# Perceiver layer on one Trainium2 core: shared expert with stationary weights, expert weights halved in place, fp32 down weights

## The reference

```python
x = x + cross_attention(layernorm(x), ctx, ctx)   # 16 heads of 16, 257 keys
x = x + attention(layernorm(x))                   # normalised weights, q and k; mixed with its input
x = x + moe(layernorm(x))

def moe(xt):                                      # xt [1024, 256]
    logits = xt @ gate_w.T                        # 8 experts
    idx = top_k(logits + beta, 2)
    c = scatter(sigmoid(logits[idx]))
    g = xt @ gate_proj_w[e]; u = xt @ up_proj_w[e]     # [256, 512] each
    eo = (silu(g) * u) @ down_proj_w[e]                # [512, 256]
    shared = (silu(xt @ shared_gate_w) * (xt @ shared_up_w)) @ shared_down_w
    return sum_e(c_e * eo_e) + shared
```

## Time and profile before

| | us |
|---|---|
| median of 3 runs (lowest, highest) | 446.9 (444.79, 455.19) |
| the profiled execution's own time | 446.99 |
| its span, first to last instruction | 445.2 |
| busy: TensorE matmuls | 366.0 |
| busy: GpSimd | 248.3 |
| busy: VectorE, ScalarE | 235.3, 235.2 |

### The profile page before, as it was taken

How to read it: one execution, slowest core, us unless ns; L and a number is a source line. 1 busy time by engine, 2 the same in 40 slices (tenths; PEclk the granted TensorE clock), 3 DMA queues, 4 the chain that set the end, 5 groups by cost and what they waited for, 6 DMA issues and landing times.

```text
span 445.2 us, 8817 instructions
## 1 busy us (share of the span) xinstructions
PE 366.0 (82%) x3020; PEld 245.2 (55%) x3020; DVE 235.3 (53%) x498; ACT 235.2 (53%) x478; POOL 248.3 (56%) x316
## 2 busy tenths in 40 slices
PE   4679978989898879788579676777779999999991
PEld 3356646667675556555467563443435656556660
DVE  1744456556555864686763746965642333333330
ACT  3546875757676666675585753455432332333330
POOL 4258588988765984855253515577293233242332
PEclk9979999999999998998898888999998999999998
DMA  7444958595779878566912112068742434454231
GB/s 221 148 93 92 179 124 174 122 173 130 156 195 219 193 166 203 121 131 130 353 50 96 49 49 78 17 205 285 245 87 51 62 49 64 57 61 61 39 35 24
DMA packets 110570, 55.54 MB, mean 125 GB/s; under 512 B 85920, under 2 KB 104352, under 8 KB 110528
## 3 DMA queue, kind: packets, MB, share of 16 engines
q1 hardware_dynamic: 106336, 49.66, 48.1%
q0 software_dynamic: 4192, 5.32, 7.6%
HBM read 21.51 MB, written 9.33 MB: 69 GB/s over the span
## 4 chain that ended last, share of the span: by engine, by line
PE 27%; DVE 22%; DMA 21%; ACT 13%; issue 11%; POOL 5%; POOLq 0%; SPq 0%; ACTq 0%; DVEq 0%
PE bank L1203 18%; DMA out<-yrow,info 18%; PE quad L1203 6%; ACT prob L605 4%; DVE cat L784 3%; ACT kT L584 2%; DMA pT<-p 2%; DVE negmax L815 2%; POOL wdn L477 2%; DVE qm L802 2%; ACT v_hi L513 2%; DVE qk L784 2%; DVE wgu L921 1%; POOL p L423 1%; DVE v_lo L784 1%
## 5 line engine op out<-in xcount | busy, mean ns | idle before, releaser
L605 ACT ACTIVATE prob<-quad,negmax 128x257 f32<-128x257 f32 x128 | 54.1, 481 | 49.2 <-DVE negmax L815 48.8
L423 POOL TENSOR_TENSOR p<-prob,p 128x512 f16<-128x512 f32 x64 | 72.8, 1138 | 5.3
L506 POOL DMA_INDIRECT out<-yrow,info x23 | 36.0, 1564 | 70.6 <-DMA out<-yrow,info 60.4
L420 POOL TENSOR_SCALAR p<-prob 128x512 f16<-128x512 f32 x64 | 41.3, 645 | 49.9 <-DMA pT<-p 30.5
L1203 PE MATMUL quad<-wgu,xT 128*128 x276 | 63.8, 381 | 1.5 <-issue 1.1
L784 DVE TENSOR_TENSOR v_lo<-bank,v_hi 128x512 f16<-128x512 f32 x32 | 22.1, 691 | 61.1 <-ACT v_hi L513 61.1
L1203 PE MATMUL bank<-cT,wk 128*128 128x257 f32 x128 | 43.6, 430 | 7.5 <-DMA cT<-in_ctxT 5.9
L1203 PE MATMUL quad<-kT,qm 64*128 64x257 f32 x256 | 44.6, 428 | 3.5 <-ACT prob L605 3.5
L815 DVE TENSOR_REDUCE negmax<-quad 128x2 f32<-128x514 f32 x64 | 42.5, 684 | 6.2 <-PE quad L1203 6.2
L784 DVE TENSOR_TENSOR hT<-bank,hT 128x512 f16<-128x512 f32 x31 | 21.4, 690 | 44.0 <-ACT hT L513 44.0
L1203 PEld LDWEIGHTS quad<-wgu,xT 128*128 128x128 f16 x276 | 26.8, 98 | 32.1 <-issue 6.7
(11 more groups left out here) (206 smaller groups left out, 743.1 us busy)
## 6 DMA issues: line engine op xcount, KB each, us to landing
wide<-un SPq DMA_DIRECT2D x32, 132.0 KB, 2.9
cT<-in_ctxT SPq DMA_DIRECT2D x8, 514.0 KB, 4.1
wst<-in_L_ffn_gate_proj_w SPq DMA_DIRECT2D x8, 512.0 KB
wst<-in_L_ffn_up_proj_w SPq DMA_DIRECT2D x8, 512.0 KB
wst<-in_L_ffn_down_proj_w SPq DMA_DIRECT2D x8, 512.0 KB
routed_rows<-pad_row SPq DMA_DIRECT2D x1, 3036.0 KB, 12.8
pT<-p SPq DMA_TRANSPOSE x64, 3.5
out<-acc SPq DMA_DIRECT2D x8, 128.0 KB
```

Source lines behind the costliest of these rows:

```text
L420: pool.tensor_scalar(out=p16[n % 2][:, h, 0, :, :], in0=prob[n % 4][:, h2, 0:256], scalar1=1.0, scalar2=0.0, op0=ALU.mult, op1=ALU.add).th ...
L423: pool.tensor_tensor(out=p16[n % 2][:, h, 1, :, :], in0=prob[n % 4][:, h2, 0:256], in1=p16[n % 2][:, h, 0, :, :], op=ALU.subtract).then_in ...
L506: pool.indirect_dma_start(out, bass.IndirectOffsetOnAxis(ap=info[n % NR][:, 0:1].bitcast(I32), axis=0), yrow[n % 2][:, :], None, compute_o ...
L605: act.activation(prob[m % 4][:, g, :], quad[:, g, 0:LK], ACT.Exp, bias=negmax[m % 4][:, g:g + 1]).then_inc(exps, 1)
```

## The change

1. The four staging buffers go. There are 18 slots `wslot` of 4 KB a partition; the fp32 gate or up chunk c is loaded into slot c + 2 and its two fp16 halves are written to slot c. The shared gate and up use `sslot` in the same way. All 16 gate and up chunks are halved by ScalarE (`high`) and VectorE (`w_low`), two in each of the 8 shared tiles; the shared ones during the self attention. GpSimd halves nothing.
2. Down weights, routed (`wdn`) and shared (`sdn`), stay fp32 and are loaded straight to their place. `down` is 4 fp32 matmuls of 256 columns.
3. Shared tiles: the weights are stationary and the tokens stream, in 4 blocks of 128 hidden columns, 6 matmuls of 128 columns each, so that `hid` comes out transposed and is itself the stationary operand of `down`. No turn, no copy.
4. Routed tiles: up and turn as before; ScalarE copies the turned tile once, as fp32, and VectorE's low half goes.
5. `xr16` is filled by eight transposing DMAs of SyncE from `x16` (`rows_back`) instead of 16 GpSimd instructions.
6. Loads: two in the attention loop; ten and the pad write from its end; six after the last cross-attention tile; the eight downs after the rows.
7. Order: on TensorE the logits of all tiles stand ahead of the first shared half; `down(q)` stands ahead of `up_half(q + 2)`; on VectorE `up(q + 2)` stands last in a shared tile's turn. `od` moves from wide to qm. R, PARTS and NJ are 128, 1 and 23: the tiling of routed rows is unchanged.

```diff
-        wdn = sb("wdn", [P, NE, 2, 4, E], F16, sc)
+        wdn = sb("wdn", [P, NE, 4, E], F32, sc)
-        wst = [sb(f"wst{i}", [P, 2 * M], F32, sc) for i in range(NC)]
+        wslot = sb("wslot", [P, 2 * NE + 2, 2, 2, M], F16, sc)
+        sslot = sb("sslot", [P, 4, 2, 2, M], F16, sc)
+        sdn = sb("sdn", [P, 4, E], F32, sc)
...
+                def gate_up(c):
+                    e, n = divmod(c, 2)
+                    w = a[("L0_ffn_gate_proj_w", "L0_ffn_up_proj_w")[n]][e].rearrange("(k p) m -> p k m", p=P)
+                    sp.dma_start(whole(wslot[:, c + 2, :, :, :]).rearrange("p (k m) -> p k m", k=2), w).then_inc(ld_u[c // 4], 16)
+                def rows_back(q):
+                    sp.wait_ge(xl_ok, 2 * q + 2)
+                    for a_ in range(2):
+                        for k in range(2):
+                            sp.dma_start(xr16[:, 4 * q:4 * q + 4, a_ * E + k * P:a_ * E + (k + 1) * P], x16[a_][:, k, 4 * q * P:(4 * q + 4) * P],
+                                         transpose=True).then_inc(xr_in, 16)
...
-                    if 16 <= n < 20:
-                        expert_part(n - 16)
-                    elif 22 <= n < 25:
-                        expert_part(n - 18)
+                    if n in (24, 26):
+                        shared_part((n - 24) // 2)
+                for c in range(4):
+                    gate_up(c + 12)
+                sp.wait_ge(U_ps, B)
+                for c in range(5):
+                    gate_up(c)
+                sp.dma_start(sdn[:, :, :], ...).then_inc(ld_sd, 16)
+                for j in range(4):
+                    sp.wait_ge(un_out[j], 16 * NT)
+                gate_up(5)
                 sp.wait_ge(pool_k, 2)
                 sp.dma_start(xs_dram.rearrange("(j p) e -> p j e", p=P), ...).then_inc(xs_pad, 16)
+                sp.wait_ge(WO_ps, NT)
+                for c in range(6, 12):
+                    gate_up(c)
+                rows_back(0)
+                sp.wait_ge(W2_ps, NT)
+                rows_back(1)
+                for e in range(NE):
+                    sp.dma_start(wdn[:, e, :, :], ...).then_inc(ld_wd, 16)
...
-                for t in range(NT):
-                    pool.wait_ge(n3_rows, t + 1)
-                    pool.tensor_scalar(out=xr16[:, t, 0:E], in0=xn[:, t, :], ...)
-                    pool.wait_ge(row_hi, t + 1)
-                    pool.tensor_tensor(out=xr16[:, t, E:2 * E], ...)
+                pool.wait_ge(xr_in, 16 * 8)
...
+                def high(c):
+                    if c % 4 == 0:
+                        act.wait_ge(ld_u[c // 4], 64)
+                    wait(act, w_lo, c - 1)
+                    act.activation(halves(wslot[:, c, :, :, :], 0), whole(wslot[:, c + 2, :, :, :]), ACT.Copy, scale=SH).then_inc(w_hi, 1)
...
                 for q in range(NT + TILES):
+                    if q + 2 < NT:
                         silu(q + 2)
+                    if q < NT:
+                        high(2 * q)
+                        high(2 * q + 1)
...
                 for q in range(NT + TILES):
                     if q < NT:
+                        w_low(2 * q)
                         y_(q)
+                        w_low(2 * q + 1)
                     if 0 <= q + 1 - NT < TILES:
                         sel_(q + 1 - NT)
+                    if q + 2 < NT:
+                        up(q + 2)
+                    elif NT <= q + 1 < NT + TILES:
+                        up(q + 1)
...
+                        for c in range(4):
+                            cols = slice(c * P, (c + 1) * P)
+                            i = 0
+                            for k in range(2):
+                                for a_, w_ in ((0, 0), (1, 0), (0, 1)):
+                                    last = mm(dst[:, cols], sslot[:, n, w_, k, cols], x16[a_][:, k, q * P:(q + 1) * P], i == 0, i == 5)
+                                    i += 1
...
+                    for c in range(4):
+                        if q < NT:
+                            last = mm(bank[6 + s][:, 0:E], hid[s][:, c * P:(c + 1) * P], sdn[:, c, :], c == 0, c == 3)
+                        else:
+                            w = wdn[:, bass.ds(te[q - NT][0], 1), c, :].rearrange("p a n -> p (a n)")
+                            last = mm(bank[6 + s][:, 0:E], hT[s][:, c * P:(c + 1) * P], w, c == 0, c == 3)
...
-                lg_(4)
-                lg_(5)
+                for t in range(4, NT):
+                    lg_(t)
                 up_half(0, 0)
-                lg_(6)
-                lg_(7)
...
                     down(q)
+                    if q + 2 < NT:
+                        up_half(q + 2, 0)
+                        up_half(q + 2, 1)
+                    elif q == NT - 1:
+                        expert(0)
+                        up_half(NT, 0)
+                        up_half(NT, 1)
```

More of the change, by code:

```diff
@@ L170, in perceiver_kernel @@
         acc = sb("acc", [P, NT, E], F32, sc)
-        hT = [sb(f"hT{i}", [P, 2, 4, P], F16, sc) for i in range(2)]
         yrow = [sb(f"yrow{i}", [P, E], F32, sc) for i in range(2)]
@@ L174, in perceiver_kernel @@
         hid = [sb(f"hid{i}", [P, M], F32, sc) for i in range(2)]
+        hT = [sb(f"hT{i}", [P, M], F32, sc) for i in range(2)]
         sb("spacer", [P, 376], F32, sc)
@@ L256, in vt_bank, with halves, whole @@
             return bank[(3, 3, 7, 6)[p]]
-        def gate_up(c):
-            return (NE - 1, c - 3) if c < 5 else divmod(c - 5, 2)
-        def by_pool(c):
-            return POOL_LO[0] <= c < POOL_LO[1] or POOL_LO[2] <= c
-        def nth(c):
-            return sum(by_pool(i) == by_pool(c) for i in range(c + 1))
-        def half(c, i):
-            if c < 2:
-                return sgu[:, c, i, :, :].rearrange("p k m -> p (k m)")
-            if c == 2:
-                return sdn[:, i, :, :].rearrange("p k m -> p (k m)")
-            if c >= 19:
-                return wdn[:, c - 19, i, :, :].rearrange("p k m -> p (k m)")
-            e, n = gate_up(c)
-            return wgu[:, e, n, i, :, :].rearrange("p k m -> p (k m)")
+        def halves(slot, i):
+            return slot[:, i, :, :].rearrange("p k m -> p (k m)")
+        def whole(slot):
+            return slot.rearrange("p i k m -> p (i k m)").bitcast(F32)
         def n3_bank(p):
@@ L465, in _ @@
                         bias(t + 1)
-                def halves(c):
-                    if c == 5:
-                        pool.wait_ge(U_ps, B)
-                    elif c == 11:
-                        pool.wait_ge(WO_ps, NT)
-                    pool.wait_ge(w_sc, nth(c))
-                    pool.tensor_copy(half(c, 0), wst[c % NC][:, :]).then_inc(g_hi, 1)
-                    pool.wait_ge(g_hi, nth(c))
-                    pool.tensor_tensor(out=half(c, 1), in0=wst[c % NC][:, :], in1=half(c, 0), op=ALU.subtract).then_inc(g_lo, 1)
-                for c in range(POOL_LO[0], POOL_LO[1]):
-                    halves(c)
                 pool.wait_ge(WO_ps, NT)
@@ L498, in _ @@
                                                 xr[:, t, :], None).then_inc(scat, 16)
-                for c in range(POOL_LO[2], CHUNKS):
-                    halves(c)
                 pool.wait_ge(stored, 16 * NT)
@@ L996, in _ @@
                         gate_weights()
-                    if 20 <= n < 23:
-                        w_low(n - 20)
                     if n == B - 5:
@@ L1463, in expert @@
                 def expert(k):
-                    te[k] = pe.value_load(te_i[0:1, k:k + 1], min_val=0, max_val=NE - 1)
+                    te[k] = [pe.value_load(te_i[0:1, PARTS * k + i:PARTS * k + i + 1], min_val=0, max_val=NE - 1) for i in range(PARTS)]
                 def up_half(q, n):
@@ L1499, in hidden @@
                     pe.wait_ge(hid_ok, q + 1)
-                    wait(pe, ht_lo, q)
-                    if q == 0:
+                    wait(pe, ht_out, q - NT)
+                    if q == NT:
                         pe.wait_ge(od_out, NT)
-                    for k in range(4):
-                        last = pe.transpose(bank[5][:, k * P:(k + 1) * P], hid[q % 2][:, k * P:(k + 1) * P], ident[:, :])
+                    for c in range(4):
+                        last = pe.transpose(bank[5][:, c * P:(c + 1) * P], hid[q % 2][:, c * P:(c + 1) * P], ident[:, :])
                     last.then_inc(HT_ps, 1)
```

230 lines of the change are left out of this document (87 added, 143 removed).

## The result

| | before | after |
|---|---|---|
| median of 4 runs (lowest, highest), us | 446.39 (444.79, 455.19) | 426.81 (425.04, 429.78) |
| the profiled execution's own time, and its span | 446.99, 445.2 | 425.04, 423.3 |
| busy: TensorE matmuls; VectorE; ScalarE; GpSimd | 366.0; 235.3; 235.2; 248.3 | 365.1; 204.3; 222.8; 192.4 |

The ratio of after to before is 0.958, 95% interval 0.950 to 0.966: faster. The forecast was 430 (419 to 442). TensorE's busy time has hardly changed (366.0 to 365.1), so some 21 of the 22 us are idle time taken from between its instructions.

The account below looks back on a forecast made before the run. It took TensorE to bound the routed stage, nearly level with the adding DMA chain, and waits on VectorE and GpSimd halvings earlier. Terms -4.0 - 8.0 - 6.4 + 1.7 = -16.7 took 446.99 to 430.3, said as 430 (419 to 442).

Parts of the forecast that it names:

- B: Self attention up to the logits: GpSimd's ten halvings and ScalarE's ten scalings leave; -8.0 us, bounds -3 and -13.
- C: Logits to first routed tile: earlier scatter, rows by DMA transposes, new shared tiles; -6.4 us, bounds -9 and +5.
- A: Attention loop: three first halvings and five of seven weight loads leave; -4.0 us, bounds -1 and -6.
- D: Routed tiles: fp32 down makes a tile 4.84 us, TensorE the limit; +1.7 us, bounds -1 and +6.
- The two rows of the chain give 2.5 us: Attention loop: two VectorE weight halvings in the chain of waits, 0.79 and 1.70 us, are saved.
- I take 2.0: Self attention: 2.0 us saved at the product cat's gap of 2.20, and 2.0 at the four products' gap of 4.33.
- The clock: ... 2.0: Self attention, mean clock 0.86: with gaps shortened, 3 to 4 us of work run at full speed, saving 2.0 us.
- Rival 1: Self attention's gain is given back to other waits and slow clock stays: -9.7 in all, 437.3 us; chance 0.17.
- The last halving ends near 314: End of the shared tiles: weight halvings finish near 314 us, before the first routed tile at about 317.7.
- It fits by 0.5: Shared tiles: VectorE's hid(q+2) is ready about 8.2 us after down(q) began; down(q+2) wants it at 8.7.
- Rival 3: Row transposes wait in SyncE's queue behind 12 MB of loads and pad write, scatter 35 us late: 465 us; chance 0.05.
- Rival 2: Weight loads set the shared tiles' pace, 6.4 us a tile, first routed tile 7.8 later: 438 us; chance 0.06.

Follow-up runs that it names:

- x5: after with three halvings back in the attention loop, their two loads at n = 16 and 17, and two self-attention halvings gone: 445.54 us, ratio to before 0.990.
- x3: after with four weight loads moved back into the attention loop at n = 16 to 19: 430.54 us, ratio to before 0.957.
- x1: after with GpSimd's ten halvings put back into the self attention, on spare buffers: 442.63 us, ratio to before 0.988.
- x9: after, unchanged, run again on another chip: 439.57 us, ratio to before 0.989.
- x4: after with each pair of weight halvings one shared tile earlier: 425.65 us, ratio to before 0.947.
- x7: after with only the first two of the four matmuls of each routed down: 439.49 us, ratio to before 0.972.
- x12: x4 with shared tiles streaming their weights in 512-column matmuls, in a new VectorE and ScalarE order: 423.66 us, ratio to before 0.945.

## Why the prediction was right, and where it was not

Forecast 430.3 for the profiled execution, measured 425.0; the change of -22 splits into these, read at the marks (the last low part, which the prediction's parts B and C meet at, went from 274.83 to 256.18):

| | forecast | measured |
|---|---|---|
| ahead of n = 11 | 0 | -1.2 |
| A, n = 11 to 27 | -4.0 | -4.4 |
| B, to the last low part | -8.0 | -13.0 |
| C, to the first routed up | -6.4 | -4.5 |
| D, to the end | +1.7 | +1.3 |

- **A, right in sum, wrong in its terms.** "The two rows of the chain give 2.5 us" and "The loads cost at least one wait on a late transpose ... I take 1.5". x5 and x3 give the halvings 5.5 and the loads 0.5 or less. The chain view names only what sits on the last path; in x5 the product cat came late as well, and the clock fell behind it.
- **B, the mechanism right, the size too small.** The steps that failed are "I take 2.0" at each of the gaps, and "The clock: ... 2.0". x1 gives the whole stage back (90.6 for 90.2) and, against x3 on the same chip, 12 us of the median. x9 parts the two terms: its clock from 204 to 256 was 0.87, like before's 0.86, and n = 27 to the logits took 79.2; after's own profile had 0.99 and 75.3:

```profile
204.00:256.00 52.00, 42.16 (x591) 32.79 (x589) 27.20 (x78) 29.57 (x40) 0.30 (x2) 0.87 0.59 207
```

From before's 90.2 to x9's 79.2 are 11 us. Of these 1.9 are part C's, the logits no longer behind a shared half (from the last low part to the logits 2.5 us in before, 0.65 in after). So the gaps gave 9 (forecast 6.3) and the clock, where it held, 4 (forecast 2.0). Three gaps had been priced, each from the one instruction that was seen slowed; by VectorE's 15 us in x1 the ten halvings slowed it at other places too. Rival 1 (B given back) is refuted by the products of 0.42 us and by TensorE's wait for them, 4.0 against 6.8 in x1.
- **C, a limit missed.** "First routed tile at about 317.7" was counted from the rows (314.8 + 2.7 is 317.5), 41.7 us after the logits by its own terms (317.7 less 277.35 - 1.3). The rows were there sooner, about 39.8 after them (256.8 to 296.6). The failed step is "The last halving ends near 314", 38 us after the logits: it ended 43.9 after them (300.7). The first down began 8.1 us after the logits instead of 6.5, since the shared halves ahead of it ran at half clock until 262.0, a tile took 0.13 more, and the last four halvings had no tile left to hide in. The routed up then ran at half clock, 5.30 us. x4 took this away and stands at 40.6. "It fits by 0.5" (hid) held for the first tiles and cost 1.88 once, at 295.58. Rival 3, the row transposes late in SyncE's queue, is refuted: the last was issued at 262.7, they landed in a median of 2.5 us, and the scatter began at 268.9, released by VectorE's row information.
- **The shared tile**, forecast 4.33, measured 4.46: 2.68 for 48 matmuls (0.056 each) and 1.78 for 8 records of down. Rival 2 is out. By the Trainium skill (TensorE: Matmul & The Clock Gate, Back-to-back issue gap), whose figure is about 81 ns a pair, the 48 would take 3.9, an estimate from the page; the trace does not agree, it shows 56 ns. On the chips with pauses the mean was worse than either, but by standstills and not by the spacing.
- **D, right in sum (122.4 for 122.8).** 4.84 a tile was 4.753, and the first yrow came 11.6 us after the first up, not 9.65, since the slow stretch lay on it; the two errors offset. The reading of before was off: "The routed stage ... is TensorE's own" does not hold, and "the adding chain needs 4.37" came from one add; x7 shows a chain of 4.57, so before's 4.55 was the chain.
- **The signs it named.** cat and qk at 0.42 each (1.43 for four), the first scatter, the first routed up and GpSimd's waits came out on the forecast's side, scatter and up 7 and 5 us earlier than named. One idle time ahead of qk was 2.3 us, not under 2, and the yrows are 4.753 apart, not 4.8 to 4.9. The copy of n = 31 came 7.9 us earlier (206.3 to 198.4), not 4.

Two things in the good total are luck. In A and in D two wrong terms offset each other, and C's shortfall hid 1.9 of B's excess of 5. And no case of the forecast had the pauses: on the chip of x9 the same kernel takes 439.57, above the forecast's own range of 423 to 437 though inside 419 to 442, and the change is worth 1.1%; x7's stage says the same of the second chip.

## What to carry to other kernels

Work on GpSimd that nobody waits for can be the costliest work in a stage: look for a VectorE instruction on the critical path that lasts several times its usual, and for the clock that falls after the gap. When an expensive stage is tightened, the last of the background work (here the weight halvings) becomes what the next stage waits for; start it one step earlier. Measure on more than one chip before a few per cent are believed. Where two forms of a matmul are about level, the one with fewer and longer instructions is worth a try on a chip that shows such pauses; x12 was not run on one.

## What the hardware showed that was not expected

- TensorE's pauses: groups of mostly 1 to 5 matmuls, most starts 0.74 or 1.4 us apart, for 11 to 17 us, on two of the chips, 12 us of the whole time, while the DMA engines were busy at 0.36 to 0.8 and GpSimd's issues ran on undisturbed.
- GpSimd's scatter issues wait for VectorE's weight halvings. In after, ten of the sixteen start while a halving runs, and each of these ends 0.84 or 0.85 us after that halving ends (1.15 to 1.69 us long); five others take 0.97, though a halving starts during them, and the first takes 1.12. One of the ten:

```profile
278.80 1.22 DVE L889 SCALAR_TENSOR_TENSOR wslot<-wslot 128x1024 f16<-128x1024 f32 x1 [1.17 <-ACT wslot L542]
279.45 1.41 POOL L477 DMA_INDIRECT routed_rows<-xr,sl_i  x1 [0.30 <-issue]
```

In x9, where the pauses keep VectorE from its halvings, six start so, with the same 0.84 to 0.86, and the median issue is 0.97.
- A matmul with its own weight load at 128 columns costs 56 ns, one of 512 columns 217: a shared half is 24 x 0.056 = 1.3 us in the one form and 6 x 0.217 = 1.3 in the other.
